# A fused Mamba-style mixer and attention block on one core: B and C projected as one tile and spread by DMA; in attention, the feed-forward transposes moved to step 18, statistics moved behind other pieces of a step, and the token norm shared by GpSimd and VectorE

## What is computed

```
# layer 1: state-space mixer + MLP (32 sequences)
proj = rms(x) @ in_proj.T ;  z, u, B, C, dt = split(proj)      # 512, 512, 16, 16, 8
u, B, C = silu(depthwise_conv4(u, B, C) + conv_b)
B, C = B / |B|, C / |C| ;  dt = softplus(dt + bias)
z_t = (z + dt*(B u - A y)) / (1 + dt^2 A) ;  y_t = y + dt*z_t ;  out_t = y_t . C_t
x1 = x + (out + D u) * silu(z) @ out_proj.T ;  x1 + gelu(rms(x1) @ fc1.T) @ fc2.T
# layer 2: attention, 16 heads of 64 with one shared key/value head, and a gated MLP
q = ln(x) @ Wq ; k, v = ln(context) @ Wkv ; softmax(q k + mask) v @ Wout + (silu(gate) * value) @ W2
# layer 3: relu(x @ w1.T + b1) quantized to fp8 @ w2.T, result quantized
```

## Time and profile before

| | |
|---|---|
| median of 3 runs | 1746.35 us (1742.54 to 1747.15) |
| the profiled execution | 1751.45 us, of which the span of its instructions is 1749.6 us |
| mixer, one group in the steady stretch | 67.8 us (L405 at 374.19 and at 441.94) |
| attention, one group | 134 to 136 us |
| busy shares | PE 92%, DVE 73%, ACT 56%, POOL 31% |
| matmul clock | 0.965 of full on the mean |

### The profile page before, as it was taken

One profiled execution on the slowest core, in us unless ns is written; L12 is line 12 of the kernel. 1 busy time (PEld: TensorE's weight loads), 2 busy tenths in 40 slices (PEclk: granted clock), 3 DMA queues, 4 the chain that ended last, 5 costly groups with the idle time before them and its releaser, 6 DMA issues.

```text
span 1749.6 us, 35590 instructions
## 1 busy us (share of the span) xinstructions
PE 1604.0 (92%) x13256; PEld 972.1 (56%) x13256; DVE 1275.5 (73%) x3633; ACT 983.7 (56%) x2326; POOL 542.9 (31%) x689
## 2 busy tenths in 40 slices
PE   4589999999999988799899899999999999999997
PEld 2356666667666744345455455455555455455476
DVE  6879889889895766666766766766766766856745
ACT  3434634635534255575665675675676666666652
POOL 3858768767776100120101101011011011011001
PEclk8688999999999988899999999999999999999999
DMA  4000010000001434443334334234334334333210
GB/s 140 11 12 12 11 33 12 22 24 21 22 2 41 156 88 102 139 101 89 76 87 107 71 86 108 72 80 102 86 78 98 90 75 100 87 82 91 63 28 22
DMA packets 177613, 119.24 MB, mean 68 GB/s; under 512 B 113856, under 2 KB 171136, under 8 KB 176544
## 3 DMA queue, kind: packets, MB, share of 16 engines
q1 hardware_dynamic: 176976, 116.50, 26.3%
q10 hardware_dynamic: 464, 0.46, 0.1%
HBM read 96.92 MB, written 7.42 MB: 60 GB/s over the span
## 4 chain that ended last, share of the span: by engine, by line
PE 70%; DVE 19%; issue 3%; DMA 3%; POOL 3%; ACT 2%; SPq 0%; DVEq 0%; POOLq 0%; ACTq 0%
PE ps L1633 18%; PE ps L1624 10%; PE ps L1588 8%; PE ps L1608 8%; PE ps L387 3%; PE ps L314 3%; PE ps L405 3%; DVE m_u L727 3%; PE ps L440 2%; PE ps L1693 2%; DVE m_rs L759 2%; PE ps L427 2%; PE ps L373 2%; POOL x_xs L1375 2%; DVE x_blk L1978 1%
## 5 line engine op out<-in xcount | busy, mean ns | idle before, releaser
L1964 DVE CUSTOM_DVE_ANT_0 x_pr<-ps,x_mk 128x375 f32<-128x375 f32 x448 | 226.3, 542 | 201.5 <-PE ps L1588 146.8
L1845 ACT ACTIVATE x_pr<-x_pr,x_rc 128x375 f32<-128x375 f32 x448 | 247.1, 599 | 148.8 <-DVE x_rc L1970 148.8
L1839 ACT ACTIVATE x_pr<-x_pr,x_mx 128x375 f32<-128x375 f32 x448 | 266.3, 595 | 111.4 <-DVE x_mx L1964 111.0
L1978 DVE STREAM_TRANSPOSE x_blk<-x_pr 128x384 f32<-128x384 f32 x448 | 232.0, 556 | 24.5 <-ACT x_pr L1845 24.5
L1544 POOL TENSOR_TENSOR x_cT<-x_cT,x_rb 128x375 f32<-128x375 f32 x64 | 57.1, 914 | 606.5 <-DMA x_rb<-context_roots 606.5
L1633 PE MATMUL ps<-x_xn,x_w 128*128 128x448 f32 x512 | 217.8, 564 | 5.3 <-DVE x_ff L2029 5.3
L1588 PE MATMUL ps<-x_kT,x_qT 64*128 64x375 f32 x896 | 178.7, 509 | 3.3 <-ACT x_kT L1888 3.3
L1608 PE MATMUL ps<-x_blk,x_va 32*64 32x224 f32 x6144 | 166.2, 358 | 12.9 <-DVE x_blk L1978 11.8
L1608 PEld LDWEIGHTS ps<-x_blk,x_va 32*64 32x64 f32 x6144 | 137.0, 133 | 55.0 <-issue 51.0
L1633 PEld LDWEIGHTS ps<-x_xn,x_w 128*128 128x128 f32 x512 | 95.7, 196 | 104.2 <-issue 82.6
L314 PE MATMUL ps<-m_xa,w_in 128*128 128x448 f32 x352 | 147.7, 567 | 6.2 <-ACT m_xa L532 6.2
(11 more groups left out here) (205 smaller groups left out, 2764.7 us busy)
## 6 DMA issues: line engine op xcount, KB each, us to landing
x_mk<-in_mask SPq DMA_DIRECT2D x224, 187.5 KB, 2.7
x_va<-x_vT SPq DMA_DIRECT2D x256, 48.0 KB, 2.1
x_cx<-in_context SPq DMA_DIRECT2D x32, 375.0 KB
x_cT<-in_context_turned SPq DMA_DIRECT2D x32, 375.0 KB, 3.7
x_rb<-context_roots SPq DMA_DIRECT2D x32, 187.5 KB, 4.5
m_Rd<-bc_roots SPq DMA_DIRECT2D x8, 448.0 KB, 3.6
x_mixed<-m_x SPq DMA_DIRECT2D x8, 448.0 KB, 3.8
X<-x_mixed SPq DMA_DIRECT2D x8, 448.0 KB, 4.1
```

What stands on the lines that cost most here:

```text
L1839: act.activation(pr[:, k, 0:J], pr[:, k, 0:J], ACT.Exp, scale=-1.0, bias=mx[:, k:k + 1], accum_out=sums[:, k:k + 1]).then_inc(h_e.sem, 1)
L1845: act.activation(pr[:, k + e, 0:J], pr[:, k + e, 0:J], ACT.Copy, scale=rc[:, k + e:k + e + 1]).then_inc(h_n.sem, 1)
L1964: dve.tensor_tensor_reduce(pr[:, k + e, 0:J], bank(SCORE_BANKS[p % NP] + e)[:, 0:J], mk[:, p % SLOT, :], -1.0, 3.0e38, ALU.add, ALU.min, m ...
L1978: dve.transpose(blocks[:, place_of(p), e, :, :].rearrange("p c x -> p (c x)"), pr[:, 2 * (p % SLOT) + e, :]).then_inc(h_t.sem, 1)
```

## The change

Mixer: B and C become one tile (64 rows of B, 64 of C, each state repeated for 4 heads). NT is 10. PE has one `bc_tile` per group, the one in `scan` before the last `scan_out`; the one behind `scan` is gone. ACT and DVE do one tap tile, one tanh, one silu, one square. The result stands in `bc` (half of r2), and SP copies it with four DMAs per group (two halves of B, two of C, 64 partitions each) into BCa, which has the old form. DVE's `scale_bc` waits for them. Attention: `ftoken` in step 18 in place of 17; seats of query 3, query 4 and down 1; `context_stats` between X and Y; `tokens_norm(it, 0)` behind Y; POOL norms sequences 0 and 1 and DVE sequences 2 and 3.

```diff
-NT = 3 + 2 * KI
+NT = 2 + 2 * KI
+    bc = r2[:, 0, :, :].rearrange("p b s -> p (b s)")
-    bsq = r1[0:64, 0, :, :].rearrange("p b s -> p (b s)")
+    bsq = r1[:, 0, :, :].rearrange("p b s -> p (b s)")
...
+        def spread_bc(i):
+            sp.wait_ge(a_si.sem, a_si.value(i, 1))
+            hold(sp, a_L, i - 1, 2)
+            for c in range(2):
+                for g in range(2):
+                    sp.dma_start(BCa[64 * g:64 * g + 64, c, :], bc[64 * c:64 * c + 64, :]).then_inc(c_in.sem, 16)
...
+        spread_bc(0)
         spread_roots(0)
         for i in range(NG):
             if i < LAST:
+                spread_bc(i + 1)
                 spread_roots(i + 1)
...
             if i + 1 < NG:
-                bc_tile(i + 1, 1)
+                bc_tile(i + 1)
             scan_out(GB - 1)
...
             scan(i)
-            if i + 1 < NG:
-                bc_tile(i + 1, 2)
             out_project(i, i + 1 < NG)
...
         def bc_parts(i):
-            hold(act, a_L, i - 1, 2)
-            tap(i, 0, 1, BCa[:, 0, :])
-            tap(i, 1, 2, BCa[:, 1, :])
+            hold(act, a_R, i - 1, a_R.per)
+            tap(i, 0, 1, bank(0), bc)
             hold(act, a_si, i - 1, a_si.per)
-            tanh_half(i, 0, BCa[:, 0, :], a_cv, 3)
-            tanh_half(i, 1, BCa[:, 1, :], a_cv, 6)
-            hold(act, a_R, i - 1, a_R.per)
-            for c in range(2):
-                act.wait_ge(a_si.sem, a_si.value(i, c + 1))
-                at = slice(32 * c, 32 * c + 32)
-                act.activation(bsq[at, :], BCa[at, c, :], ACT.Square).then_inc(a_bsq.sem, 1)
+            tanh_half(i, 0, bc, a_cv, 3)
+            act.wait_ge(a_si.sem, a_si.value(i, 1))
+            act.activation(bsq, bc, ACT.Square).then_inc(a_bsq.sem, 1)
...
         def bc_parts(i):
-            taps(i, 0, 1, BCa[:, 0, :])
-            taps(i, 1, 2, BCa[:, 1, :])
-            silu(i, 0, BCa[:, 0, :], BCa[:, 0, :])
-            silu(i, 1, BCa[:, 1, :], BCa[:, 1, :])
+            taps(i, 0, bank(0), bc)
+            silu(i, 0, bc, bc)
...
+            dve.wait_ge(c_in.sem, c_in.value(i + 1, 0))
             dve.wait_ge(r_in.sem, r_in.value(i + 1, 0))
...
-        at[17, "X"].append(("ftoken", n))
+        at[18, "X"].append(("ftoken", n))
...
-SEAT = {"gate": (1,) * 8, "value": (3,) + (0,) * 7, "out": (1, 0), "kv": (2,) * 4, "query": (1, 1, 0, 0, 1, 0, 2, 3),
-        "back": (2, 3), "ftoken": (2, 3), "token": (2, 3), "down": (3, 1), "up": (1, 0) * 4}
+SEAT = {"gate": (1,) * 8, "value": (3,) + (0,) * 7, "out": (1, 0), "kv": (2,) * 4, "query": (1, 1, 0, 1, 0, 0, 2, 3),
+        "back": (2, 3), "ftoken": (2, 3), "token": (2, 3), "down": (3, 2), "up": (1, 0) * 4}
...
-            rooted(pool, 0, lambda b: token(X, it + 1, b), lambda b: xs[:, b, :], x_nm)
+            rooted(pool, 0, lambda b: token(X, it + 1, b), lambda b: xs[:, b, :], x_nm, range(GH))
...
-                if r == CONTEXT[0] and not (last and b >= 2):
-                    context_stats(it + (b + 2 > GB), (b + 2) % GB)
-                if p == TOKENS[0] and not last:
-                    tokens_norm(it, 0)
...
                 parts(it, p, "X", first, last)
+                if r == CONTEXT[0] and not (last and b >= 2):
+                    context_stats(it + (b + 2 > GB), (b + 2) % GB)
                 parts(it, p, "Y", first, last)
+                if p == TOKENS[0] and not last:
+                    tokens_norm(it, 0)
+                if p == TOKENS[2] and not last:
+                    dve.wait_ge(c_ln.sem, c_ln.value(it + 1, CROOT))
+                    filled(dve, it - 1, ("token", 1))
+                    rooted(dve, 0, lambda b: token(X, it + 1, b), lambda b: xs[:, b, :], x_nm, range(GH, GB))
```

More of the change, by code:

```diff
@@ L305, in turn_tokens @@
             else:
-                hold(pe, a_cv, i - 1, 3 * 4)
+                hold(pe, a_cv, i - 1, 3 * 3)
             for k in range(KD):
@@ L320, in dt_tile, with bc_tile @@
             in_tile(0, bank(6)[:, 0:T])
-        def bc_tile(i, n):
+        def bc_tile(i):
             hold(pe, b_mc, i - 1, 6)
-            in_tile(n, bank(n - 1)[:, 0:T])
+            in_tile(1, bank(0)[:, 0:T])
         def gate_tiles(i):
             hold(pe, b_mc, i - 1, 8)
[L328 to L332, removed]
+            for m in range(KI):
+                if m == 2:
+                    pe.wait_ge(a_cv.sem, a_cv.value(i, 3))
+                in_tile(2 + m, bank((2 + m) % 4)[:, 0:T])
+                if i == 0 and m == 1:
                     column_means(pe)
-                if n == 4:
+                if m == 1:
                     squared_sums(i)
@@ L338, in squared_sums @@
             hold(pe, b_yt, i - 1, b_yt.per)
-            pe.wait_ge(a_bsq.sem, a_bsq.value(i, 2))
+            pe.wait_ge(a_bsq.sem, a_bsq.value(i, 1))
             for b in range(GB):
-                last = pe.matmul(bank(5)[0:S, 2 * b:2 * b + 2], bsq[:, b * S:(b + 1) * S], heads_of, start=True, stop=True)
+                last = pe.matmul(bank(5)[0:S, 2 * b:2 * b + 2], bsq[:, b * S:(b + 1) * S], states_of, start=True, stop=True)
             last.then_inc(a_bst.sem, 1)
@@ L345, in u_tiles @@
             for m in range(KI):
-                pe.wait_ge(a_si.sem, a_si.value(i, 3 + m))
-                in_tile(3 + KI + m, bank((2 + m) % 4)[:, 0:T])
+                pe.wait_ge(a_si.sem, a_si.value(i, 2 + m))
+                in_tile(2 + KI + m, bank((2 + m) % 4)[:, 0:T])
                 if i == 0 and m == 1:
@@ L548, in step_relu, with tap @@
             act.activation(relu, bank(6)[:, 0:T], ACT.Relu, bias=dtb).then_inc(a_abs.sem, 1)
-        def tap(i, c, n, dst):
+        def tap(i, c, n, src, dst):
             act.wait_ge(a_proj.sem, a_proj.value(i, n + 1))
-            act.activation(dst, bank((n - 1) % 4)[:, 0:T], ACT.Identity, scale=cw[:, c, TAPS - 1:TAPS], bias=conv_b[:, c:c + 1]).then_inc(a_tap.sem, 1)
+            act.activation(dst, src[:, 0:T], ACT.Identity, scale=cw[:, c, TAPS - 1:TAPS], bias=conv_b[:, c:c + 1]).then_inc(a_tap.sem, 1)
         def tanh_half(i, m, src, ready, k):
@@ L578, in u_taps @@
             for m in range(KI):
-                tap(i, 2 + m, 3 + KI + m, ua[:, m, :])
+                tap(i, 1 + m, 2 + KI + m, bank((2 + m) % 4), ua[:, m, :])
         def u_part(i, m):
-            tanh_half(i, 2 + KI + m, ua[:, m, :], a_cv, 9 + 3 * m)
+            tanh_half(i, 1 + KI + m, ua[:, m, :], a_cv, 6 + 3 * m)
         def turned_u(i):
@@ L717, in scaled_b, with taps @@
                 dve.tensor_scalar(xs[:, b, :], x1[:, i % XR, b, :], rr[:, GB + b:GB + b + 1], None, ALU.mult).then_inc(b_nv.sem, 1)
-        def taps(i, c, n, dst):
+        def taps(i, c, src, dst):
             dve.wait_ge(a_tap.sem, a_tap.value(i, c + 1))
-            src = bank((n - 1) % 4)[:, 0:T].rearrange("p (b s) -> p b s", s=S)
+            src = src[:, 0:T].rearrange("p (b s) -> p b s", s=S)
             acc = dst.rearrange("p (b s) -> p b s", s=S)
@@ L735, in bc_parts @@
         def bc_parts(i):
-            taps(i, 0, 1, BCa[:, 0, :])
-            taps(i, 1, 2, BCa[:, 1, :])
-            silu(i, 0, BCa[:, 0, :], BCa[:, 0, :])
-            silu(i, 1, BCa[:, 1, :], BCa[:, 1, :])
+            taps(i, 0, bank(0), bc)
+            silu(i, 0, bc, bc)
         def gate_part(i, m):
-            silu(i, 2 + m, bank((2 + m) % 4)[:, 0:T], zg[:, m, :])
+            silu(i, 1 + m, bank((2 + m) % 4)[:, 0:T], zg[:, m, :])
         def u_parts(i):
@@ L746, in u_parts @@
                 if m < KI:
-                    taps(i, 2 + m, 3 + KI + m, ua[:, m, :])
+                    taps(i, 1 + m, bank((2 + m) % 4), ua[:, m, :])
                 if m >= 1:
-                    silu(i, 2 + KI + m - 1, ua[:, m - 1, :], ua[:, m - 1, :])
+                    silu(i, 1 + KI + m - 1, ua[:, m - 1, :], ua[:, m - 1, :])
         def softplus(i):
@@ L1370, in place_of, with rooted @@
         return tile_of(p) + AHEAD_BY * (p // NP % 2)
-    def rooted(eng, g, src, dst, done):
-        for b in range(GB):
+    def rooted(eng, g, src, dst, done, which=range(GB)):
+        for b in which:
             eng.tensor_scalar(dst(b), src(b), mv[0:S, GB * g + b, 0:1], rt[0:S, 1, g, b:b + 1], ALU.subtract, ALU.mult).then_inc(done.sem, 1)
```

32 lines of the change are left out of this document (16 added, 16 removed).

## The result

The changed kernel takes 1704.28 us (median of 4 runs, 1700.69 to 1705.84) against 1746.75 us of the kernel before on the same chip: a ratio of 0.9758, 95% interval 0.9735 to 0.9781, so 42 us less. The prediction was 1704. The profiled execution of the changed kernel took 1705.84 us, its span is 1704.0 us. Against the 1749.6 us of before that is 45.6 us; the profile of before was a somewhat long execution, 4.7 us above its median, this one is too, by 1.6 us.

A forecast was written before the change was run, and what follows sets the result against it. PE was taken to bound the mixer, meeting DVE twice per group, and PE's 5.2 us of gaps to be winnable in attention. C tile 11.3, steps 17 to 21 14.4 + 1.3, token norm 8.3, clock 6.8: 1746.35 - 42.1 = 1704, range 1692 to 1722.

The forecast's parts named there:

- C tile: Mixer, PE: dropping the separate tile of C saves 1.61 us in each of 7 groups, 11.3 us.
- the meeting at the turn of u: Mixer, each group: DVE's last silu of u ends at 410.96 and PE's turn of u starts at 411.02.
- A mixer group of 66.2: Mixer: sign that the forecast is right, a group of 66.2 us with PE as full as now.
- Copies: Mixer: the four DMAs of B and C land 8 us before DVE wants them and cost nothing.
- Start-up: Mixer start: the first scan waits 9.48 us for POOL's `right`, so DVE's 2.8 us saved there give nothing.
- Steps 17 to 21: Attention: moving the feed-forward transposes brings the product with v 2.4 us earlier per group, 14.4 us in six groups.
- Token norm: Attention: splitting the norm between POOL and DVE starts the token transposes 1.4 us earlier, 8.3 us in 6 groups.
- Rival 1: Attention, token norm: POOL and DVE collide, DVE's two take 1.4 us each, 12.5 us less gain, 1716.5; 7%.
- Seats: Attention: new seats for queries 3 and 4 and down 1 give nothing, since PE doesn't wait there.
- The clock: Attention: without waits over 1.2 us, four slow stretches at half clock return 1.7 us each, 6.8 us.
- The sum: Whole kernel: 11.3 + 14.4 + 1.3 + 8.3 + 6.8 = 42.1 us less, giving 1704 us.
- DVE and ACT set the pace: Attention rival: steps 17 to 21 return only 1.3 us, step 24 1.0, clock dips stay; 25.6 us, 1721; 18%.

The follow-up runs named there:

- E5: Changed kernel plus one tile of four products on PE where the tile of C stood; ratio 0.9786 to the kernel before.
- E6: Changed kernel with the four copies of B and C issued behind the roots' two transfers instead of ahead; ratio 0.9816 to the kernel before.
- E9: Changed kernel with the statistics of context and tokens back ahead of the step's parts on DVE; ratio 0.9753 to the kernel before.
- E3: Changed kernel with the feed-forward transposes back in step 17; median 1727.47 us, ratio 0.9877 to the kernel before.
- E4: Changed kernel with all four sequences of the token norm on GpSimd again; ratio 0.9810 to the kernel before.
- E7: Changed kernel with DVE's two token norm sequences moved directly behind the roots in step 22, beside GpSimd's two; median 1702.14 us, ratio 0.9741 to the kernel before.
- E11: As E7, with GpSimd's two norm instructions replaced by products of the tokens with themselves; ratio 0.9759 to the kernel before, two runs.
- E10: Changed kernel with queries 3 and 4 and the second down tile on their old banks; ratio 0.9744 to the kernel before.
- E2: Old mixer with the changed attention; ratio 0.9796 to the kernel before, 35.6 us less.
- E12: As E7, with PE's key and value tile behind the other tile of step 19 instead of ahead; ratio 0.9752 to the kernel before.
- E8: Changed kernel with all four token norm sequences on DVE directly behind the roots in step 22, GpSimd none; ratio 0.9768 to the kernel before.
- E1: Changed mixer with the old attention; ratio 0.9944 to the kernel before, 9.8 us less.

## Why the prediction was right, by its steps

- *C tile, 1.61 us in 7 groups, 11.3*: 1.61 in its own stretch, and E5 shows it from the other side. The 11.1 us of the seven groups are near to 11.3 by luck: they hold six of the tiles, at 1.9 us a group in these two traces, less 0.4 in the last group. Over the ten kernels with the new mixer unchanged the first six groups take 65.8 to 66.4 us each, mean 66.0, the two with the old one 67.8 and 67.7: 1.7 a group, near 12 us with the seventh tile. What the step lacked is that the meeting at the turn of u, which it had seen, goes one way or the other with the slow silus, 0.7 us in some groups. "A mixer group of 66.2" lies between the 65.8 without them and the 66.4 to 66.6 with them.
- *Copies, nothing, 8 us of slack*: about 10 us. The warning that each us beyond the cover costs 7 nearly holds by E6: 2.0 us late in the first six groups and 3.1 in the last cost 10.9 and 4.4 us.
- *Start-up, nothing*: 1.9 us in these two traces, of which 1.6 are the seventh C tile, counted above. The first scan starts at 81.0 and 81.1 us in the two traces with the old mixer and at 79.9 to 80.6 in the twelve with the new one, so some 0.8 us were there to be had; the spread behind it, below, hides them.
- *Steps 17 to 21, 2.4 us a group*: 2.52, PE's small waits 0.33, 0.62 and about 0.1 for the 0.35, 0.85 and 0.4 predicted. But one sentence was wrong: that without the transposes both waits of PE, 2.58 and 1.03, could go, and that the statistics "only change places". E9 shows that the order of the statistics removes the second wait, and that it is worth 1.06 us of a group; E3 gives 1.7 to 2.2 us to the transposes. With E4's 1.36 these are 4.1 to 4.6 us for a difference of about 3.9 to 4.2 between groups without slow tiles. The sum was right since both were in the same step.
- *Token norm, 1.4 us*: the wait went from 1.83 to 0.45, and E4 gives 1.36. The limit that I put on it, a collision for which 0.3 us was the margin, is not there: E7 overlaps the two engines and pays 0.12 us, not 2.1. Rival 1 had the wrong price, taken from the earlier trace rows, where POOL's partner was a product of two tensors (at 592.39 in the trace before, 1.30 us). The rule cited from the Trainium skill, SBUF — State Buffer, section "SBUF: two separate sides", names an instruction of GpSimd that reads SBUF as the partner for VectorE's two-operand instructions and any GpSimd one for the 2-port modes; by it either pair of E7 and E11 would have cost the same, if DVE's instruction ran in such a mode, and neither pair anything, if it did not. The trace agrees with the first for E11, and for the silus with what it says of two operands, but not for E7; with the second it agrees for E7 and not for E11 or the earlier trace rows.
- *Seats, nothing*: E10.
- *The clock, 6.8 us*: the slow stretches are gone, from 750 to 1650 us, in every trace without the wait of 2.58 us (the changed kernel, E2, E4 to E12), back in E3. In three traces with that wait the stretches are 4, 5 and 6; of these, three stand behind a wait for POOL's norm, of 1.83, 1.84 and 2.18 us, so 2.58 us is not the condition for each. That they don't come behind 1.8 us alone rests on one trace, E4's.
- *The sum*: five periods between token transposes, less three slow stretches of 1.69, are 3.87 us shorter each; I had 3.8. Not foreseen were 1.3 us in group 0, and 0.9 of the 2.2 us behind group 6; 3.1 us in group 1 where I had 3.8. With 13.0 us ahead of attention for 11.3 that makes the 45.6 us of the two spans, 3.5 more than forecast. That the medians agree with the forecast within 0.3 us is luck, since the interval of their ratio is 8 us wide.
- *DVE and ACT set the pace* (18%) was the wrong forecast and half the truth for the next step: E7, E8 and E12 each take a wait from PE and make no group shorter, and in each PE waits for DVE's turn at the next product with v.

## What to carry to other kernels

Count an instruction at the engine's own duration only in a stretch whose two ends both belong to that engine; the tile of 1.61 us cost 1.60 a group in E5. Where two engines meet within 0.3 us, the next wait removed on one of them can be worth nothing, as three times here. Before adding up a saving by groups, look where in the order each piece of it stands: one of the seven tiles stood ahead of the first landmark. And when a part is too small for the total, compare the period of the same landmark over many groups: here it tells about half a us where the medians tell 3.

## What the runs showed that I had not expected

- *A collision depends on what GpSimd does.* One and the same DVE tensor-scalar instruction takes 0.41 us alone (1.38 for four in a row), 0.46 opposite GpSimd's tensor-scalar, 0.70 opposite a GpSimd product of 0.61, and 1.36 opposite one of 1.30. A scalar-tensor-tensor of DVE with both operands in SBUF takes 0.61 to 1.5 us opposite POOL's products; with one of them in PSUM (the gates' silus) it took 0.62 throughout, though POOL had a product beside 16 of the 32.
- *The spread of the runs sits at two places.* The first output projection starts between 97.3 and 102.7 us in the fourteen traces, with little there but the granted clock of the first scan to tell them apart, beside the extra tile of 1.6 us in three of them and the 1.2 us by which the scan's start differs: from the scan's start to the first output projection it is 0.67 to 0.90 in the mean, and, the extra tile apart, the higher it is, the shorter the stretch (16.1 to 20.5 us; the scan's first part takes 8.27 us in the changed kernel and 7.27 in E3, both released by the same wait of 9.5 us). The mixer's last group takes 63.8 to 68.5 us in the ten kernels where its work is the same. Two things make that: PE's last turn of u waits 1.8 to 4.3 us for DVE's last silu, and behind the wait the clock falls in seven of the ten (from the turn to the scan it is 15.2 to 16.2 us in place of 14.0). Why DVE comes sooner or later there, I can't say. Together that is more than the 5 us between the runs of one kernel.
- *The length of the wait doesn't tell whether the half clock follows.* Behind the wait of 2.58 us, always of that length, 3 of 7 next tiles were slow before, 3 of 7 in E1, 6 of 7 in E3. Behind the wait at the mixer's last turn of u it followed 2.31 us before, and did not follow 2.75 us in E4. I found nothing that tells ahead which.
